# Cross-attention and expert layers: one fixed order instead of rounds that meet, keys reloaded by two pairs of heads, expert weights applied after the down projection

## The reference, cut to what matters

```python
attn = softmax(einsum('bhnd,bhmd->bhnm', q * scaling, k))       # layer 0: 256 x 1601, 16 heads
h = silu(x_flat @ ew1[e].T) * (x_flat @ ew3[e].T)               # layer 0: 9 experts of 352
out = out + cw[:, e:e + 1] * (h @ ew2[e].T)
scores = einsum('bqhd,bqkhd->bqkh', q, k) * SCALE               # layer 1: 64 picked rows
eo = einsum('eti,eih->eth', silu(g) * u, w_down); out = einsum('te,eth->th', combine, eo)
out = out + sigmoid(x @ shared_gate_w.T) * so                   # layer 1: 8 experts of 176 and a shared one
```

## Time and profile before

| | us |
|---|---|
| median of 3 runs | 1859.62 (1852.22 to 1864.69) |
| the profiled execution | 1863.21, of which span 1861.5 |

### The profile page before, as it was taken

One profiled execution on the slowest core, in us unless ns is written; L12 is line 12 of the kernel. 1 busy time (PEld: TensorE's weight loads), 2 busy tenths in 40 slices (PEclk: granted clock), 3 DMA queues, 4 the chain that ended last, 5 costly groups with the idle time before them and its releaser, 6 DMA issues.

```text
span 1861.5 us, 34997 instructions
## 1 busy us (share of the span) xinstructions
PE 1488.8 (80%) x13168; PEld 851.4 (46%) x13168; DVE 1194.4 (64%) x2460; ACT 896.3 (48%) x2074; POOL 726.9 (39%) x1135
## 2 busy tenths in 40 slices
PE   4178788888987888887988788888888879788966
PEld 3123463336633574335733465335743357334834
DVE  4177367557876578656776578665786567765734
ACT  4157326562366524663266633665246722665231
POOL 3235215632266223652156331662236521563051
PEclk8689889898999999998999999999999989999987
DMA  7410140003200040002300041000400022000000
GB/s 212 75 28 2 37 61 19 1 2 75 44 1 2 23 74 23 2 1 50 52 19 2 7 73 39 1 2 27 70 6 1 2 53 44 2 2 8 10 1 4
DMA packets 49754, 53.69 MB, mean 29 GB/s; under 512 B 5802, under 2 KB 38964, under 8 KB 49588
## 3 DMA queue, kind: packets, MB, share of 16 engines
q1 hardware_dynamic: 49588, 51.45, 14.0%
HBM read 38.98 MB, written 12.46 MB: 28 GB/s over the span
## 4 chain that ended last, share of the span: by engine, by line
PE 38%; DMA 26%; DVE 12%; ACT 10%; POOL 6%; issue 5%; SPq 2%; ACTq 0%; POOLq 0%; another core or an unknown queue 0%; DVEq 0%
DMA k_parts<-big 16%; DMA kst<-k_parts 7%; PE ob L663 7%; PE b L649 6%; ACT probs L942 5%; DVE mx L1117 5%; PE a L635 4%; PE b L555 3%; DMA k1st<-k_parts 3%; DVE mx L1139 2%; POOL big L1388 2%; ACT big L948 2%; PE ob L504 2%; PE b L685 2%; PE a L791 2%
## 5 line engine op out<-in xcount | busy, mean ns | idle before, releaser
L1117 DVE TENSOR_REDUCE mx<-a 128x2 f32<-128x802 f32 (+1 forms) x512 | 489.3, 986 | 278.0 <-PE a L635 275.6
L942 ACT ACTIVATE probs<-b 128x512 f32<-128x512 f32 (+1 forms) x896 | 459.0, 564 | 151.8 <-PE b L649 135.9
L663 PE MATMUL ob<-probs,vaug 128*9 128x256 f32 (+1 forms) x3328 | 284.1, 392 | 3.6 <-ACT oT L884 3.6
L1371 POOL TENSOR_TENSOR big<-iotab,idx_lo 128x512 bf16<-128x512 bf16 x256 | 274.1, 1093 | 7.7
L987 ACT ACTIVATE big<-a 128x256 f32<-128x256 f32 (+2 forms) x304 | 116.1, 382 | 324.3 <-PE a L792 321.5
L649 PE MATMUL b<-big,kst 64*128 64x256 bf16 (+1 forms) x1664 | 173.5, 278 | 106.9 <-ACT big L948 48.0
L635 PE MATMUL a<-kst,qa 64*128 64x401 bf16 (+1 forms) x1024 | 175.6, 344 | 78.2 <-SPq L474 33.7
L1234 DVE SCALAR_TENSOR_TENSOR big<-big,a 128x256 f32<-128x256 f32 (+2 forms) x304 | 127.1, 418 | 128.0 <-ACT big L987 126.2
L1352 POOL CAST qst<-nm 128x4 bf16<-128x4 f32 x64 | 15.6, 244 | 409.8 <-DVE nm L1104 409.0
L1319 POOL TENSOR_TENSOR rstd<-veps,neg_half 128x2 f32<-128x2 f32 x32 | 22.6, 705 | 367.8 <-DVE veps L1035 367.7
L649 PEld LDWEIGHTS b<-big,kst 64*128 64x128 bf16 (+1 forms) x1664 | 63.2, 95 | 220.4 <-ACT probs L942 107.9
(11 more groups left out here) (262 smaller groups left out, 2435.1 us busy)
## 6 DMA issues: line engine op xcount, KB each, us to landing
kst<-k_parts SPq DMA_DIRECT2D x96, 200.1 KB
k_parts<-big SPq DMA_DIRECT2D x24, 400.2 KB, 14.5
ctx_sb<-in_ctx SPq DMA_DIRECT2D x8, 768.0 KB
k1st<-k_parts SPq DMA_DIRECT2D x96, 32.0 KB
k_parts<-kpart SPq DMA_DIRECT2D x24, 64.0 KB, 1.6
kst<-in_L_ffn_w SPq DMA_DIRECT2D x1, 1408.0 KB
x<-in_x SPq DMA_DIRECT2D x8, 128.0 KB, 2.2
out<-x SPq DMA_DIRECT2D x8, 128.0 KB, 8.0
```

The costliest lines, as they stand in the source:

```text
L663: m = pe.matmul(ob[q:q + V1, 0:NQ], vaug[0:kn, c, 2 * p + hh, :], probs[0:kn, (2 * g + hh) % NPS, (c % 2) * NQ:(c % 2 + 1) * NQ], start=(j ...
L942: act.activation(probs[0:kn, (2 * n + hh) % NPS, 0:w], bs[(e + hh) % 3][0:kn, 0:w], ACT.Exp).then_inc(f_read, 1)
L1117: dve.tensor_reduce(mx[:, p % 2, s, :, j], bank[:, :].rearrange("p (h k) -> p h k", h=2)[:, :, 0:w], AX, ALU.max, negate=True).then_inc(m_ ...
L1371: m = pool.tensor_tensor(onehot[:, own % 2, q:q + QG, :], iotab[:, :].unsqueeze(1).to_broadcast([P, QG, P]), idx_lo[:, QG * n:QG * (n + 1) ...
```

## The change

The program is rewritten around one list of events for the whole launch (`order()`): each event of each batch gets a place on a common scale and the list is sorted by it. The scale only sets the order. All engines walk this list; there are no rounds, no `meet` and no clearing of semaphores. In particular:

- `part` 0 to 11 of the next batch stand among the last expert chunks of this one; the 56 groups follow directly. The rest of the parts come at 0.82 of a group.
- The next batch's context transposes and key projections are woven into the attention stage (a key piece every 6 groups), each piece of 512 columns is split on POOL and stored by itself, and `kst` is reloaded in four quarters (two pairs of heads each, 12 DMAs of 50 KB), each as soon as its pairs were used. The layer 1 keys and values (`key` 4, `kv1`) come near the end of the attention stage.
- `sel`, `cwT` and the transposes of the weights are gone. A chunk never spans two experts: layer 0 has 27 chunks (9 x 128, 128, 96), layer 1 has 14 (9 whole ones and 5 for the tails of 48). When an expert's chunks are done, PE makes its whole down product (`dn`) and DVE adds it, times the routing weight, to `x` (two operations of 128x128).
- DVE does two operations per chunk. `a0`, `a1` are one four-bank tile `um`, in which every part, gate/up pair, `dn` and side product takes the bank or two free longest.
- The layer 1 pair chain has one spacing everywhere, 4.4 places, also where it runs alone. The counts go by 8 queries (16 times). In batch 0 each score group has one extra PE product on constants (`keep_clock(1)`).

```diff
-            return steps, Sides(sorted(events, key=lambda e: e[0]))
+                for c in range(NP // 2):
+                    put(prep + (48 if c < 3 else XL + 1.5), "rel", b, c)
+                for k in range(NH0):
+                    put(own - 9.9 + 0.82 * k if k < 12 else own + 0.82 * (k - 12) + 0.1, "part", b, k)
+                for p in range(NP):
+                    put(own + NG * p - (0.8 if p == 0 else 4.2), "q0", b, p)
...
+                    put(prep + 20.4 + 6 * n, "key", b, n)
...
+                for p in range(NP):
+                    for d, kind in ((0, "pair1"), (2.05, "q1"), (3.05, "s1"), (3.6, "mu"), (6.05, "w1"), (7.05, "c1")):
+                        put(chain + 8.7 + 4.4 * p + d, kind, b, p)
```

```diff
-                dve.tensor_tensor(hid[0:n, u % 4, :], hu[0:n, u % 3, :], cb_bank[u % 2][0:n, 0:NQ], ALU.mult).then_inc(hid_ready, 1)
+                    for s in range(NS):
+                        m = dve.scalar_tensor_tensor(out=X[:, s, :], in0=bank[:, s * P:(s + 1) * P], scalar=cw[l][:, s, e:e + 1], in1=X[:, s, :],
+                                                     op0=ALU.mult, op1=ALU.add)
```

More of the change, by code:

```diff
@@ new lines, in build @@
+        EV = order()
+        fill, slot, rel, place, u_free, serial = {}, {}, {}, {}, {}, {}
+        nfill = nslot = nrel = 0
+        for ev in EV:
+            kind, b, n = ev
+            if kind in F_NEED:
+                fill[ev] = nfill
+                nfill += F_NEED[kind]
+            if kind in M_NEED:
+                slot[ev] = nslot
+                nslot += 1
+            if kind in M_NEED or kind == "hd":
+                rel["gu" if kind == "hd" else kind, b, n] = nrel
+                nrel += 1
+            group = "norm" if kind in ("n4a", "n1a", "n2a", "n3a") else "le" if kind in ("le0", "le1") else kind if kind == "key" else None
+            if group:
+                serial[ev] = (group, 1 + sum(1 for g in serial.values() if g[0] == group))
@@ new lines, in build @@
+        seen, last = 0, [-1] * 4
+        for ev in EV:
+            kind = ev[0]
+            if kind in M_NEED or kind == "gu":
+                need = M_NEED.get(kind, 1)
+                at = [range(k, k + need) for k in range(5 - need) if max(last[k:k + need]) < seen]
+                own = min(at, key=lambda r: (kind == "gu" and last[r[0] ^ 1] < seen, max(last[k] for k in r)))
+                u_free[ev] = max(last[k] for k in own) + 1
+                place[ev] = list(own)
+                for k in own:
+                    last[k] = rel[ev]
+            if kind in M_NEED or kind == "hd":
+                seen += 1
@@ L633, in max_part, with scores @@
+            def scores(b, g):
+                p, j = divmod(g, NG)
+                e = fill["s0", b, g]
+                if j == 0:
+                    pe.wait_ge(f_read, fill["q0", b, p] + 1)
+                own = [free_fill(e), free_fill(e + 1)]
+                if b == 0:
+                    keep_clock(1, own[0])
+                for c in chunks(j):
+                    kn = rows(c, NK)
                     for hh in range(2):
                         o = SLOT * hh
-                        m = pe.matmul(bank[:, hh * MMAX:hh * MMAX + n], qa[o:o + SLOT, p, s, :],
-                                      kst[o:o + SLOT, p, j * KM:j * KM + n], start=True, stop=True)
@@ new lines, in down @@
+            def down(b, e):
+                l, own = divmod(e, NE)
+                bank = free_slot(("dn", b, e))
+                pieces = down_pieces(l, own)
+                pe.wait_ge(u_read, rel["gu", b, max(u for u, _, _, _ in pieces)] + 1)
+                w = (w2T, wd_sb)[l]
+                for s in range(NS):
+                    for k, (u, r0, r1, at) in enumerate(pieces):
+                        m = pe.matmul(bank[:, s * P:(s + 1) * P], hid[r0:r1, (NCH * b + u) % NHID, s * P:(s + 1) * P], w[r0:r1, at, :],
+                                      start=(k == 0), stop=(k == len(pieces) - 1))
+                m.then_inc(m_psum, 1)
@@ L996, in _ @@
-            for l in range(2):
-                act.wait_ge(sel_part, l + 1)
-                for t in (1, 2):
-                    copy(sel[l][CWP * t:CWP * t + NE, :], sel[l][0:NE, :]).then_inc(sel_done, 1)
             for g, (dst, srcs) in enumerate(stages):
@@ L1302, in _ @@
[L1302 to L1312 removed]
+            dve.wait_ge(pre_dve, 9)
@@ L1443, in _ @@
[L1443 to L1455 removed]
+            pool.wait_ge(pre_dve, 9)
```

1663 lines of the change are left out of this document (711 added, 952 removed).

## The result

The changed kernel takes 2048.28 us (median of 4 runs, 2039.96 to 2052.08), the kernel before beside it 1858.64 (4 runs): 1.1015 times as long, 95% interval 1.0964 to 1.1066. It is 10% slower where 2% less was forecast. The profiled execution has a span of 2048.2 us against 1861.5.

The account below looks back on a forecast made before the run. PE, busy 80% of the span, was taken as the bound, its gaps as what can be won. Terms -16 - 10 - 27 + 13 = -40 took 1863 to 1823 us; forecast 1785 to 1855 (0.53), 8-in-10 range 1745 to 1880.

Parts of the forecast that it names:

- The share of the DMA chain: Key reload: 26% of the chain but nearly all beside full PE work; removing it gives about 1 us a round.
- Ahead of batch 0: Before the first score group: keys reloaded in quarters, first group near 95 instead of 111.3, -16 us.
- Routing without the split: Expert stage: without POOL's key split beside it, routing takes 3.5 us, PE's gap and slow clock go; -8.5 a round.
- Weights out of the chunks: Expert chunks: PE work +1.5 us a round, +3 for nearly equal PE and DVE, -3 for the dropped weight transpose.
- Parts among the last chunks: End of expert stage: the 12.4 us block goes, 9.5 comes back among the last 13 chunks; -2.9 us a round.
- Keys into the attention stage: Key projections and splits moved: expert stage -3.6 us, attention stage +9 a round, between bounds 0 and 20.
- The query transpose: Attention stage: pair 1's transpose stands right behind its last part in PE's list; +1 us a round.
- Round 0: Batch 0: attention +17 us (constants 12, keys 5), shorter expert stage; -10 taken for the round.
- Layer 1 alone: End of last batch: small steps behind the multiplication close a loop, a pair takes 6.1 us instead of 3.56; +18.
- the last batch, its experts: Last batch's expert stage: no transposed weights needed; -4 us.
- The slower one: Attention stage: POOL bounds it, a stage grows by 20 rather than 10 us, kernel at 1893; chance 0.17.
- The rival of hidden work: Attention stage: woven key work fills PE's idle time, +9 becomes +1, kernel about 1765; chance 0.25.

Follow-up runs that it names:

- four_keysback: As four_tail, with the next batch's four key pieces in the expert stage and all four reload quarters behind them; 1826.11 us, ratio 0.9857.
- place_oldest: The changed kernel with each gate/up pair taking the bank freed longest ago, without the preference for a busy bank's neighbour; 2003.42 us.
- three: The changed kernel with query transposes 2.0 places ahead, oldest-freed bank for gate/up, and the last batch's first pair products up to 5.9 places earlier; 1942.56 us.
- three_block: As three, with the first twelve parts of a batch in one block behind the last gate/up pair; 1935.72 us.
- four_tail: As four_small, with w1 and c1 of the last batch 1.65 places later, behind the next pair's scores; 1889.20 us.
- q0_later: The changed kernel with the query transposes of pairs 1 to 7 set 2.0 places ahead of their first score group instead of 4.2; 1975.24 us.
- four_small: As three_block, without batch 0's constant products, and the last batch's first pair products only 1.5 places earlier; 1928.33 us.
- q0_filled: The changed kernel with six constant PE products ahead of each query transpose of pairs 1 to 7; 2038.17 us.

## Why the prediction was wrong, step by step

A middle round was forecast 4.5 us shorter and became 22.4 us longer, 26.9 apart. Of these the edits account for some 23: 7.9 at the query transposes, 6.6 at the bank of a gate/up pair, 4.1 at the woven parts, 4.1 at the keys.

**The share of the DMA chain: right.** DMA went from 26% of the chain to 1% and the kernel got slower all the same. What the reload gave by itself was not measured; four_keysback has it back beside the experts and is the fastest.

**Ahead of batch 0: right.** First part forecast near 82, measured 82.28; first score group forecast near 95, measured 94.74.

**Routing without the split: right.** No 18-number operation takes more than 0.27 us there, and PE's gap of 7.6 us is gone; the longest one up to layer 0's first chunk is 1.3. From the last score group to layer 0's first gate/up product the stage went from 40.4 us to 31.9 (means of batches 1 to 6). The forecast's terms for this part make about -10.5: -8.5 for the routing, +3, -3, -3.6, and 1.6 for layer 1's chunks. place_oldest brings it to 29.3, so the missing 2 us were, roughly, waits for banks, theory D's cause.

**Weights out of the chunks: the cost was right, the hand-over was not seen.** 3.93 us an expert was right, once the bank was right. The changed kernel took 4.82, and 5.0 to 5.8 with side products. The prediction's last sentence ("if the four-bank tile makes PE wait in the chunk stretches") names it, but it had no chance and no price. The rule that chooses the bank stands in the code and could have been walked through for three chunks. One of the term's sums is off as well: PE's 23.7 us in layer 1's stretch is not what its own 12.0 and 8.1 make, 20.1.

**Parts among the last chunks: nothing gained.** -2.9 forecast; +1.2 measured in the stage against a block (three against three_block).

**Keys into the attention stage: mechanism right, size under.** +9 and -3.6 forecast; taking the key pieces out again gives -13.1 and +3.2. The 9 was to hold the context transposes and more counts besides. The term named the bank that each new fill takes from the scores, and that is what the waits at `ACTq L859` are. It left the granted clock where the earlier trace rows showed it, at 1.00 with PE busy 83%. In these runs the clock did not stay: the stages are at 0.82 to 0.92 in four_tail and at 0.93 to 0.97 in four_keysback.

**The query transpose: +1 forecast, 9 measured** (144.9 to 136.0). This is the step that failed most. The diff had the transposes' place for every pair; I counted one wait where there are two or three a stage (4.6 to 6.5 us), and no clock behind them.

**Round 0: +17 forecast, +34.8 measured.** The constants cost 12 to 18, as said, where 12 were taken. The later transpose gave 7.3 of it back (q0_later, 109.2), and moving the keys 8.6 (four_tail to four_keysback, 95.5 to 86.9).

**Layer 1 alone: right in its loop, short in size, blind to a second one.** 6.1 forecast, 6.85 measured. The closed loop of the prediction is what the rows of the changed kernel show. Its scores and first exponential take about 2.3 us where 1.6 were taken, and 0.6 of that is the 1.2 GHz level: L616 and L620 take 1.01 and 0.60 us there, 0.61 and 0.39 in four_tail. What the prediction did not see is `w1` ahead of the next scores, which ends only 0.2 us earlier. four_small would have been my repair, and it makes a pair 2.3 us longer. The other miss of the last batch, its experts (+11.1 where -4 was forecast), is for the most part the bank: place_oldest has 10.3 us less there.

**The rivals.** The slower one named the attention stage (at 1893), rightly, but its mechanism, POOL as the bound, is not what happened: POOL is busy 58% there, and cutting its splits gave 27 us of 190. The rival of hidden work (0.25) fell too, and so did the forecast's whole range. No chance was given to a low clock, though the expert stages of before show how it follows a gap.

What is not settled: from four_keysback's 124.4 us to the 120.1 of before the attention stage keeps 4 us, and 0.93 to 0.97 of the clock. Which of the smaller edits (counts by 8 queries, layer 1 keys, first chunks in the stage) holds them was not tried. Nor is the low clock itself explained: the runs show it behind idle pieces of PE, and filling the transposes' idle time raised it only to 0.93 or 0.94.

## What to carry to other kernels

When events are put on a scale and sorted, look at each wait of the bottleneck engine and ask what stands ahead of it on the other engines and what useful work stands behind it; a transpose or a product that waits belongs as late as its reader allows. Price added work at the clock that the stage will have: here 46 us of waits of 2 us each cost 73. Where two chains close a loop nearly together, moving one gives nothing, and can cost. A rule that assigns buffers is part of the order; walk it before pricing a pipeline by its instructions.

## What the runs showed of the hardware that was not expected

**Idle time and the clock.** The same 1150 PE instructions took 138.2 us at 0.93 and 147.2 at 0.84. Filling idle places with constant products (q0_filled) did not make the kernel slower, 2048 to 2038 us, though PE did more; 56 such products ahead of batch 0's score groups cost 12 to 18 us.

**A split beside VectorE does not stretch every operation.** The 18-number operations of before went from 0.18 to 2.87 us. VectorE's one-hot comparison (bf16, SBUF to SBUF) in the changed kernel takes 0.42 us where POOL is idle and 1.15 beside POOL's multiplication and the subtraction behind it, which end at 814.8 and 815.9:

```profile
813.89 1.15 DVE L1052 TENSOR_SCALAR big<-big 128x1024 bf16<-128x1024 bf16 x1
822.09 0.42 DVE L1052 TENSOR_SCALAR big<-big 128x1024 bf16<-128x1024 bf16 x1
```

In four_keysback a chunk's operations, which read PSUM, run beside the split that begins on POOL at 595.13 and lasts 1.16:

```profile
595.39 0.41 DVE L1036 SCALAR_TENSOR_TENSOR th<-th,um 112x256 f32<-112x256 f32 x1
595.84 0.42 DVE L1038 TENSOR_TENSOR hid<-th,um 112x256 f32<-112x256 f32 x1
```

They take what they take elsewhere, 0.41 and 0.42. The Trainium skill, GPSIMD Engine Reference, section Key points, has GpSimd contend with VectorE operations that run in a two-port mode or have two SBUF inputs; the two pairs of rows agree with that, for the chunk's operations have one input in PSUM. So the splits could go beside the chunks, and not beside the routing. They are not free there either: a normalisation that reads SBUF (L919) takes 0.34 us alone and up to 1.31 beside POOL in four_keysback.
